# Two transformer layers on one core: score work in steps of four heads, and one ring of eight PSUM banks

## The reference

```
# layer 0 attention: 16 heads of 8 features, softmax over all 256 keys
qkv = x @ Wqkv + bqkv; q, k, v = split(qkv per head)
out = softmax(q k^T / sqrt(8)) v;  x = LN(x + out @ Wproj + bproj)
# layer 0 feed-forward: 128 -> 512, butterfly of 9 stages, exact gelu, butterfly, 512 -> 128
x = LN(x + butterfly(gelu(butterfly(x @ W_exp + b_exp) + up_bias)) @ W_con + b_con + down_bias)
# layer 1 attention: low-rank q and kv, rotary embedding, causal mask, 16 query heads on 4 kv heads
q = rope(x @ Wqa @ Wqb); k, v = x @ Wkva @ Wkvb; k = rope(k)
x = LN(x + softmax(causal(q k^T / sqrt(8))) v @ Wout + bout)
# layer 1 feed-forward: integer weights times 1/127
x = LN(x + (silu(x @ wg.T) * (x @ wu.T)) @ wd.T)
```

## Time and profile before

| | us |
|---|---|
| three runs | 358.34, 358.35, 355.75 (median 358.34) |
| the profiled execution: its own time | 358.65 |
| the profiled execution: span from first to last instruction | 356.5 |
| busy: TensorE matmul / VectorE / ScalarE / GpSimd | 331.8 / 251.3 / 188.5 / 177.8 |
| mean granted clock of TensorE, share of full | 0.989 |

### The profile page before, as it was taken

The page is one execution under the profiler, slowest core; times in us unless marked ns, Lnnn a source line. Parts: engine busy times, 40 slices in busy tenths (PEclk is TensorE's granted clock), DMA queues, the critical chain, the costliest instruction groups (busy, mean ns, idle before and its releaser), DMA issues.

```text
span 356.5 us, 10245 instructions
## 1 busy us (share of the span) xinstructions
PE 331.8 (93%) x3796; PEld 230.5 (65%) x3796; DVE 251.3 (70%) x941; ACT 188.5 (53%) x396; POOL 177.8 (50%) x299
## 2 busy tenths in 40 slices
PE   8979999999999999999999898899999999999963
PEld 4657666665647665675657656587777767676652
DVE  4655577677758777586856677468788888883374
ACT  2427666565694655746575445825546455556310
POOL 6684443230303327054542979229696956365451
PEclk9989999999999999999999999989999999999999
DMA  7463420200001010201102011110111110000000
GB/s 259 146 164 54 95 85 17 47 4 3 10 24 33 4 31 2 62 3 33 34 20 42 4 32 33 32 31 3 33 47 33 48 31 17 3 18 4 17 15 29
DMA packets 9469, 14.27 MB, mean 40 GB/s; under 512 B 2140, under 2 KB 5196, under 8 KB 9292
## 3 DMA queue, kind: packets, MB, share of 16 engines
q1 hardware_dynamic: 8988, 13.09, 14.6%
q10 hardware_dynamic: 432, 0.53, 0.5%
HBM read 6.28 MB, written 1.05 MB: 21 GB/s over the span
## 4 chain that ended last, share of the span: by engine, by line
PE 76%; issue 7%; POOL 6%; ACT 5%; DVE 4%; DMA 1%; SPq 1%; POOLq 0%; DVEq 0%; ACTq 0%
PE SM L379 28%; PE G L565 12%; PE ST L398 5%; PE G L472 5%; PE G L485 5%; PE G L537 3%; PE G L461 3%; PE G L452 2%; PE G L545 2%; PE G L496 2%; POOL E L925 2%; PE G L507 2%; PE ST L432 2%; ACT L630 1%; ACT E L630 1%
## 5 line engine op out<-in xcount | busy, mean ns | idle before, releaser
L630 ACT ACTIVATE E<-ST 128x512 f32<-128x512 f32 (+1 forms) x256 | 125.3, 541 | 126.6 <-PE ST L398 126.3
L379 PE MATMUL SM<-QK 31*128 31x256 f32 (+1 forms) x1012 | 141.2, 377 | 5.1 <-DMA QK<-qk 2.0
L398 PE MATMUL ST<-QK 32*128 32x256 f32 (+1 forms) x1024 | 136.0, 376 | 4.4 <-ACT E L630 4.4
L379 PEld LDWEIGHTS SM<-QK 31*128 31x128 f32 x1012 | 94.7, 185 | 44.0 <-DVE mx L742 12.3
L742 DVE TENSOR_REDUCE mx<-SM 128x2 f32<-128x512 f32 x125 | 80.2, 684 | 31.8 <-PE SM L379 30.0
L398 PEld LDWEIGHTS ST<-QK 32*128 32x128 f32 x1024 | 91.0, 185 | 8.0 <-ACT E L630 6.5
L750 DVE CUSTOM_DVE_ANT_0 masked_s<-SM,mask_sb 128x256 f32<-128x256 f32 (+1 forms) x256 | 75.7, 351 | 20.0 <-PE SM L379 19.7
L932 POOL TENSOR_TENSOR at<-turned,rec 128x256 f32<-128x256 f32 x16 | 10.1, 628 | 95.2 <-DVE rec L772 95.2
L565 PE MATMUL G<-E,V 128*32 128x256 f32 x992 | 53.6, 356 | 0.5 <-POOL E L925 0.5
L925 POOL TENSOR_SCALAR_AFFINE_SELECT E<-E 128x512 f32<-128x512 f32 x64 | 39.0, 634 | 12.6 <-ACT E L630 12.6
L565 PEld LDWEIGHTS G<-E,V 128*32 128x32 f32 x992 | 28.7, 110 | 22.3 <-issue 8.1
(11 more groups left out here) (136 smaller groups left out, 415.7 us busy)
## 6 DMA issues: line engine op xcount, KB each, us to landing
QK<-qk SPq DMA_DIRECT2D x60, 64.0 KB
rs<-ry SPq DMA_DIRECT2D x16, 128.0 KB, 2.3
xb<-x_nat SPq DMA_DIRECT2D x1, 1024.0 KB, 6.0
out<-ln_g SPq DMA_DIRECT2D x8, 128.0 KB, 1.9
xt<-x_t SPq DMA_DIRECT2D x1, 896.0 KB, 6.5
wi<-wi_all SPq DMA_DIRECT2D x1, 576.0 KB, 3.7
QK<-mt SPq DMA_DIRECT2D x32, 8.0 KB
fac<-fac_u SPq DMA_DIRECT2D x1, 508.0 KB, 6.1
```

The lines of the kernel that those rows point to most:

```text
L379: ins = nc.tensor.matmul(max_bank(m)[:, cols], q, QK[rows, b % QK_RING, r, 1, keys], start=True, stop=True)
L398: ins = nc.tensor.matmul(ST[m % S_RING][:, c * T:(c + 1) * T - q0], QK[rows, b % QK_RING, r, 1, c * P:(c + 1) * P], QK[rows, b % QK_RING, ...
L630: act.activation(E[:, a % E_RING, j, 0:n], ST[m % S_RING][:, 0:n], ACT.Exp, scale=SCALE)\
```

## The change

- A step has four heads (`QUAD = 4`), so there are half as many steps, and the offsets are multiples of four. A step issues two rounds of scores one right after the other: maxima of heads g+18, g+19 with exponentials of g, g+1, then maxima of g+16, g+17 with exponentials of g+2, g+3. The lead is 16 heads. `order_of` gives the place of a maximum in this order, and all of a step's maxima come first on VectorE.
- The last four steps of exponentials, which have no maxima beside them, use all four strips at once.
- The eight banks are one ring in two halves. Round one takes the half `at`, round two the other half, and the next step swaps them. General work of a step, at most four pieces, takes the banks of its own round one: in layer 0 those of the maxima first, from step 128 on (but not in the step behind a gelu) those of the exponentials first. `take` waits for a bank's last reader as before.
- General work is dealt anew over the steps (`attention_at`, `products_at`, `values_at`, `projected_at`, `up1_at`, `ffn1_at`) and its order inside a step is changed: `mt xt xt0 up0 dn1 up1 proj v pv dn0 qk`. Batches 8 to 13 have their attention tail one step later.
- The start is written out by hand: 16 maxima, the projection of batch 1, the first turned maxima and the values of batch 0 come before step 0; the fillers are gone. Late weights are loaded two a step from step 0.
- The attention norm's output has three buffers in place of two.

```diff
-QK_RING, V_RING, E_RING, S_RING = 4, 3, 4, 3
+QK_RING, V_RING, E_RING, LN_RING, BANKS = 4, 3, 4, 3, 8
...
-LEAD = 14
-AT_QK, AT_QKIN, AT_ROPE = (-34, -40, -44), -28, -34
...
-AT_UP0, AT_GELU, AT_DN0, AT_LN0, AT_XT0 = (50, 54, 64, 66), 66, (70, 72), 74, 80
...
+QUAD, LEAD, AHEAD = 4, 16, 8
+AT_MT, HURRY = (-8, 0), BATCHES - 2
+AT_QK, AT_QKIN, AT_ROPE = (-44, -36), -28, -36
+
+AT_UP0, AT_GELU, AT_DN0, AT_LN0, AT_XT0 = (52, 52, 56, 56), 60, (64, 68), 72, 76
+
+FFN1 = {b: ((40, 40, 48), 64, 68) for b in range(NB, BATCHES)}
+FFN1.update({BATCHES - 4: ((40, 40, 48), 52, 56), BATCHES - 3: ((40, 40, 40), 44, 48),
+             BATCHES - 2: ((32, 36, 36), 44, 48), BATCHES - 1: ((36, 36, 36), 40, 44)})
...
+def attention_at(g, offset):
+
+    for b in range(BATCHES):
+        if g == H * b + offset + (QUAD if NB <= b < HURRY else 0):
+            return b
+    return None
+
+
+def products_at(g):
+
+    for b in range(BATCHES):
+        first = 8 if b < NB and b % 2 == 0 else 12
+        if g == H * b + first:
+            return 2 * b
+    b = attention_at(g, 16)
+    return None if b is None else 2 * b + 1
+
+
+AT_NORM, AT_PROJ, AT_LN, AT_XT = 20, 24, 28, 32
...
+def order_of(m):
+
+    return QUAD * (m // QUAD) + (m + 2) % QUAD + 1
...
+            def claim(task, semaphore, value, g=0):
+
+                i = claimed[0]
+                claimed[0] += 1
+                if g >= HEADS:
+                    return take(i % BANKS, task, semaphore, value)
+
+                assert i < QUAD
+                if NB * H <= g and tile_at(g - QUAD, AT_GELU) is None:
+                    i = (i + 2) % QUAD
+                return take(QUAD * (g // QUAD % 2) + i, task, semaphore, value)
...
+            def scores(maxima, exps, at):
+
+                for i, m in enumerate(maxima):
+                    take((at + i) % BANKS, ("max", m), A["max_done"], order_of(m))
+                for i, m in enumerate(exps):
+                    take((at + len(maxima) + i) % BANKS, ("exp", m), A["exp_done"], m + 1)
...
                 for long in range(2):
...
+                    for m in maxima:
+                        max_scores(m, 1 - long)
+                    for m in exps:
+                        exp_scores(m, long)
...
             for g in STEPS:
...
+                at = QUAD * (g // QUAD % 2)
+                claimed[0] = 0 if g <= HEADS else claimed[0]
+                if g + LEAD < HEADS:
+                    scores((g + LEAD + 2, g + LEAD + 3), (g, g + 1), at)
+                    scores((g + LEAD, g + LEAD + 1), (g + 2, g + 3), at + QUAD)
+                elif g < HEADS:
+                    scores((), range(g, g + QUAD), at)
```

More of the change, by code:

```diff
@@ L308, in _ @@
+            spread(1)
+            maxima(0)
+            for g in STEPS:
+                if (n := half_at(g - QUAD, AT_MT)):
+                    maxima(n)
+                if (b := projected_at(g - QUAD)) is not None and layer(b) == 0:
+                    spread(b)
+                if (b := batch_at(g, AT_QKIN, (1,))) is not None:
+                    spread(b)
+                if (b := projected_at(g - QUAD)) is not None and layer(b) == 1:
                     sp.wait_ge(A["y_out"], b - NB + 1)
@@ L343, in claim @@
                 return banks[i]
[L345 to L357, removed]
+            def claim(task, semaphore, value, g=0):
[7 more added lines that the diff above has]
+                return take(QUAD * (g // QUAD % 2) + i, task, semaphore, value)
             def max_scores(m, c):
                 b, r, j = place(m)
[L362 to L371, removed]
-                        pe.wait_ge(A["max_done"], m - 2 * S_RING + 1)
                 rows = slice(STRIP * j, STRIP * j + MAXROW)
@@ new lines, in scores, with project_group @@
+                for long in range(2):
+                    for m in maxima:
+                        max_scores(m, 1 - long)
+                    for m in exps:
+                        exp_scores(m, long)
+            def project_group(r, i):
+                bank = take(i, ("first", r), first_out, 2 * r + 1)
+                if r == 0:
+                    keys = take(i + 1, "keys", first_keys, 1)
+                    pe.wait_ge(ld["x0"], 16)
+                    pe.wait_ge(ld["first"], 32)
+                elif r == 1:
+                    pe.wait_ge(ld["groups"], 16)
+                for s in range(2):
+                    to = keys if r == 0 and s == 1 else bank
+                    ins = nc.tensor.matmul(to[:, s * T:(s + 1) * T], wfirst_sb[:, r, s, :], xt[:, 0:T], start=True, stop=True)
+                ins.then_inc(first_ps, 1)
@@ new lines, in project_values @@
+            def project_values(b, bank):
+                if b == 0:
+                    pe.wait_ge(ld["v"], 16)
+                x0 = (b % NB) * T
+                for k in range(QT):
+                    ins = nc.tensor.matmul(bank[:, k * P:(k + 1) * P], xt[:, x0 + k * P:x0 + (k + 1) * P],
+                                           wv_sb[:, :] if layer(b) == 0 else wl1[:, 2, :], start=True, stop=True)
+                ins.then_inc(A["v_ps"], 1)
+            pe.wait_ge(idle_ready, 1)
+            for i in range(2):
+                nc.tensor.matmul(banks[i][:, :], idle[:, 0:P], idle[:, :], start=True, stop=True)
@@ L576, in _ @@
                 if g == JOIN:
[L577 removed]
+                    bank = claim("join", wl1_ready, 1, g)
                     pe.wait_ge(ld["l1"], 64)
```

621 lines of the change are left out of this document (295 added, 326 removed).

## The result

The changed kernel takes 343.89 us (median of four runs, 341.1 to 346.31), the kernel before 358.35 beside it on the same chip: a ratio of 0.9581, 95% interval 0.9492 to 0.9669. The forecast was 330, the range 317 to 347. The profiled execution is the longest of the four: 346.31 us, span 344.2, granted clock 0.979; the others have spans of 342.4, 341.0 and 339.0 at 0.988, 0.989 and 0.999.

The account below looks back on a forecast made before the run. TensorE, busy 93% of the span, was taken as the bound, though not full. Start 20.5, stretch 282.4 (256.9 of work plus waits) and end 25.5 gave 328.4, with 2.15 outside 330.6, so 330 us; range 317 to 347.

Parts of the forecast that it names:

- terms 1 and 2: Steps 0 to 248: joined rounds save 13.2 us, four-strip exponentials 2.5, 26 fewer whole-array blocks of general work 5.2.
- term 3: Waits that remain or come between step 0 and the last round: 25 us, making that stretch 282 for 308.4.
- term 5: End, from the last round's start: 25.5 us for 23.9, with four exponentials first and last pv behind xt and up1.
- Gelu: Part of the waits: third piece pv waits behind gelu and table load, 1.8 us four times, 7 us.
- GpSimd: GpSimd's queue delays xt 3.5 us at step 144, 0.9 at step 112, 1.5 at step 180; together 6 us.
- VectorE in layer 1: VectorE's 15.9 us a batch exceeds TensorE's 14.8; followed through, a batch takes 16.3: 5.5 us of waits in all.
- Layer 0 with hand-offs that I can't place: VectorE has room in layer 0, but steps 24, 36, 56 are short or heavy; with unplaced hand-offs 6 us.
- Term 4: Start: batch 1's projection stands before the last eight maxima, so step 0 starts at 20.5 (bounds 18.5 and 24.2).
- rival 1: TensorE meets VectorE everywhere, VectorE standing about 0.7 us before 17 up1 steps: 12 us more, 342; chance 0.27.
- rival 4: A step's second round doesn't join because its waits come after the drain: 13 us lost, 343; chance 0.06.
- Rival 3: One ring of banks lets late readers hold up scores and maxima; 0.6 us a step gives 367 us; chance 0.07.
- Rival 2: Gelu and GpSimd waits are covered by the wider ring, 10 us of 25 remain: 315; chance 0.12.

Follow-up runs that it names:

- experiment 1: Changed kernel plus a tiny product between the two rounds of each step: whole array 362.52 us (ratio 1.0074), strips' own mode 349.85 (0.9726).
- the first trace: Profiled execution of the unaltered changed kernel, the longest of its first four runs: 346.31 us, span 344.2, granted clock 0.979.
- the other half: Changed kernel, but general work of exponentials-only steps takes the half of the banks that their round doesn't use: ratio 0.9515.
- up1 first: Changed kernel with up1 ahead of dn1 on TensorE and its gate ahead of dn1's residue on VectorE, steps 192, 208, 224, 240: ratio 0.9474.
- the strip kernel: Changed kernel plus a tiny 31-row product in the strips' own mode between each step's two rounds: 349.85 us, ratio 0.9726.

## Why the prediction was right, and where it missed

- **The direction and the range** held for the reason given: the joined rounds and blocks save more than the new waits cost. From step 0 to the last round TensorE is busy 276.6 us in place of 297.4; terms 1 and 2 forecast 20.9 less (13.2, 2.5 and 5.2), and experiment 1 gives 12.5 for the first. The range was wide, though: 343.9 lies outside the 322 to 339 that the forecast itself stood for, and 3 us from the range's end.
- **Terms 1 and 2** were right: undisturbed pieces of steps 0 to 248 come to 254.7 for 256.9.
- **The number** was 14 us too low, and the step that failed is term 3, and in a small part term 5. Term 3 says 25 us of waits; there were 42.6, of which 4.2 are half clock. Without the clock and GpSimd 0.55 us a step is left, over the 0.4 of the prediction's own sign of failing, if the waits of general pieces are counted with those of the rounds. By its own points:
 - *Gelu* was right in place and mechanism, and near in size (7.2 for 7, of which 4.8 is shown to hang on the table loads); behind the fourth it is the next step's first round that waits (0.90).
 - *GpSimd* was right at step 144 (3.5 for 3.5 in the first trace), but in six other kernels the step is 0.5 to 0.7 us shorter, and the order behind it is worth 1.5 net; the 0.9 and 1.5 of steps 112 and 180 don't show as waits for GpSimd.
 - *VectorE in layer 1* gave nearly the right batch (16.8 for 16.3) for a reason that fell. I added up VectorE's work, found it longer than TensorE's, and took the longer sum. With 2.9 us less of it the batch didn't move. Of the 2.0 us of waits in a batch 0.5 is the hand-off of up1's bank, which the same paragraph names for "a step of two up1" and which also holds for one up1 that comes last; the rest stays open. That the number came near is luck.
 - *Layer 0 with hand-offs that I can't place* is the largest miss: 14 for 6. The bound written beside it (25 with layer 1) holds it. It shows in 40.9 us for two batches, where 37 to 39 were named as a sign. 1.7 is the wait behind the empty step 36, and nearly every other step has 0.1 to 0.5 too much; where the table of waits names a releaser it is nearly always a maximum. Only 1.5 of it is shown to be the order of banks, and the cause of the rest stays open.
 - *Not in the forecast at all:* three exponentials-only steps whose general work takes the banks of exponentials (4.8 us, and some of the end), and 4.2 us of half clock.
- **Term 4**: 18.64 for 20.5. Step 0 waits for the last maxima of the start, not for the DMAs of batch 1. The 1.9 us better is that execution's: over the eight traces of the same start it is 19.4 on average, and at 19.7 to 21.0 the DMA of the turned maxima, which the term doesn't count, is what step 0 waits for.
- **Term 5**: 28.3 for 25.5. 1.4 is half clock (26.95 without it), and 1.4 the same bank order as in the exponentials-only steps (25.6 with the other half).
- **Rivals 1 and 4** came nearest in time (342, 343). Experiment 1 excludes rival 4. Of rival 1 a part is real: the hand-off through tanh and gate is there, worth 1.8 us where it was moved. In the batches of layer 1 VectorE's summed work isn't the bound. In layer 0, where most of the waits with a named releaser are for maxima, no run took work from VectorE, so there the rival isn't tested. The Trainium skill (TensorEngine Tiling (Array Packing), PSUM Bottleneck) says that after faster tiling the evacuation of PSUM may become the bound. Here it did in part, and as latency per bank: taking a fifth of VectorE's work away changed nothing, while moving one product and its readers ahead of another gave 0.5 us of a batch of 16.8.
- **Rival 3** is, in kind, some of what came on top: 42.6 us over 63 steps is 0.68 a step, of which the forecast had 0.4. The point at which nothing would be gained was put at 0.44 more; 0.28 came, clock included.
- Rival 2 (few waits remain) is out.

## What to carry to other kernels

When buffers are merged into one ring, follow each bank from its last reader to its next writer, in order of issue. An engine's summed work said little here (a fifth less changed nothing), while a bank that passes two engines behind a step's last piece cost 0.5 to 0.7 us in each of the three steps where moving the piece removed the wait. Try the piece with the longest way out first in a step and the one with the shortest last. Look at the steps that aren't like the others as well (no maxima, no general work, one half of the ring idle): a rule of turns that fits the steady state met its waits there. And before a whole run is compared with another, look at the start and at the granted clock step by step: of the 3.2 us between the profiled executions of the changed kernel and of up1 first, 1.8 is the edit.

## What the runs showed of the hardware

- A single whole-array product between two rounds in strips costs 0.21 us a step more than the same product in the strips' own mode, so mixing modes once a step was worth 12.5 us of 358.7.
- TensorE's granted clock fell to half, from 2.4 to 1.2 GHz, for stretches of 3.4 or 6.8 us in a kernel that keeps TensorE busy for 90% of its span. In the first trace they came 0.1 us behind an idle time of 1.31 us (step 128), within one of 2.97 (step 144), and behind one of 2.17 in the end. Such a stretch makes the work in it up to twice as long: 1.6 us at step 128 (9.44 against 7.81), 2.4 at step 148 (8.36 against 5.99).
- The idle time alone doesn't decide: behind waits of 1.3 to 1.5 us step 128 was at half in four traces, and behind waits of 1.0 to 1.9 at full in six. In four of these six the half clock came in step 0. The spread between executions of one kernel (341.1 to 346.3) goes with the mean clock (0.999 to 0.979); what sets it off stays open.
- One execution of the strip kernel took 599.11 us. The matmuls of a round took 630 ns on average, where they take 369 in the changed kernel, while VectorE's reductions took the same (687 and 684 ns) and the profile's granted clock reads 1.000. So that share doesn't show every slowing of TensorE. It was seen once.
